# Decoder layer on one core: three of the six cross-attention units of a batch take their exponentials head by head on ScalarE, under a new written order of the work

## The reference, cut to what matters

```
q = (queries @ Wq + bq).reshape(N, L, H, D)      # L = 112 queries
k = (keys @ Wk + bk).reshape(N, S, H, D)         # S = 375 context rows
v = (values @ Wv + bv).reshape(N, S, H, D)
sm = jnp.einsum('nlhd,nshd->nlhs', q, k) / math.sqrt(D)
sm = jax.nn.softmax(sm, axis=1)                  # over l: one maximum and one sum per (h, s)
attn = jnp.einsum('nlhs,nshd->nlhd', sm, v).reshape(N, L, H * D)
```

## Time and profile before

| | |
|---|---|
| median of 3 runs (lowest, highest) | 1372.14 us (1371.88, 1373.69) |
| the profiled execution, its own time | 1372.99 us |
| its span, first to last instruction | 1371.2 us |
| PE busy | 1220.7 us (89%) |
| DVE busy | 1140.3 us (83%) |
| ACT busy | 876.9 us (64%) |
| POOL busy | 343.0 us (25%) |

### The profile page before, as it was taken

How to read it: one execution, slowest core, us unless ns; L and a number is a source line. 1 busy time by engine, 2 the same in 40 slices (tenths; PEclk the granted TensorE clock), 3 DMA queues, 4 the chain that set the end, 5 groups by cost and what they waited for, 6 DMA issues and landing times. The chain is left out here.

```text
span 1371.2 us, 28241 instructions
## 1 busy us (share of the span) xinstructions
PE 1220.7 (89%) x8850; PEld 892.6 (65%) x8850; DVE 1140.3 (83%) x2358; ACT 876.9 (64%) x2290; POOL 343.0 (25%) x431
## 2 busy tenths in 40 slices
PE   1789999999999999999999999999976868759598
PEld 1466666666666666666666666666645757659598
DVE  6369999999999999999999999999973447868698
ACT  1366666666666666666666667666532449959695
POOL 0233432233343223333222334322210000000043
PEclk9899999999999999999999999999986989979799
DMA  5100001000000100000000000000000000000033
GB/s 161 38 20 19 19 19 31 21 18 21 18 18 18 32 18 18 21 18 18 22 29 18 18 21 18 19 26 13 4 8 4 0 0 1 0 0 1 17 101 97
DMA packets 35042, 33.07 MB, mean 24 GB/s; under 512 B 4148, under 2 KB 34604, under 8 KB 34988
## 3 DMA queue, kind: packets, MB, share of 16 engines
q1 hardware_dynamic: 32704, 31.50, 7.6%
q10 hardware_dynamic: 2284, 0.89, 0.3%
HBM read 25.04 MB, written 7.34 MB: 24 GB/s over the span
## 5 line engine op out<-in xcount | busy, mean ns | idle before, releaser
L561 ACT ACTIVATE Px<-score 125x896 f32<-125x896 f32 x192 | 176.2, 918 | 127.4 <-PE score L1080 66.1
L747 DVE TENSOR_REDUCE nmax_c<-score 125x8 f32<-125x896 f32 x192 | 208.4, 1086 | 6.0 <-PE score L1002 5.6
L729 DVE TENSOR_REDUCE Zc<-Px 125x8 f32<-125x896 f32 x192 | 206.8, 1077 | 7.9 <-ACT Px L561 4.4
L554 ACT ACTIVATE Ps<-score,nmax_s 112x112 f32<-112x112 f32 x512 | 173.6, 378 | 3.6 <-DVE nmax_s L754 3.6
L506 POOL TENSOR_TENSOR rstd<-vare,half 112x1 f32<-112x1 f32 x64 | 35.0, 548 | 474.5 <-DVE vare L839 474.5
L1080 PE MATMUL score<-sel,nmaxT 128*125 128x448 f32 x384 | 125.3, 407 | 1.8 <-ACT nmaxT L567 1.8
L554 ACT ACTIVATION_READ_ACCUMULATOR Ps<-score,nmax_s 112x1 f32 x512 | 118.8, 232 | 0.0
L1091 PE MATMUL outX<-Px,Vn 125*32 125x224 f32 x1536 | 113.4, 369 | 2.1 <-DVE Vn L740 2.1
L740 DVE TENSOR_TENSOR Vn<-Vx,rZc 125x128 f32<-125x128 f32 x192 | 112.8, 587 | 1.2
L567 ACT ACTIVATE nmaxT<-maxT 128x125 fp32r<-128x125 f32 x192 | 53.6, 279 | 89.6 <-PE maxT L1074 89.4
L1002 PE MATMUL score<-Qbd_hi,KxT_hi 64*125 64x448 f32 x384 | 90.4, 467 | 1.2 <-ACT Px L561 1.2
(11 more groups left out here) (245 smaller groups left out, 3482.3 us busy)
## 6 DMA issues: line engine op xcount, KB each, us to landing
ctx_in<-in_ctx SPq DMA_DIRECT2D x32, 375.0 KB
x_in<-in_x SPq DMA_DIRECT2D x32, 112.0 KB, 2.0
x_scratch<-x SPq DMA_DIRECT2D x32, 112.0 KB, 5.6
x2T_all<-x_scratch SPq DMA_DIRECT2D x32, 112.0 KB, 2.1
out<-x2T_all SPq DMA_DIRECT2D x32, 112.0 KB, 1.9
raw_w_up<-in_w_up SPq DMA_DIRECT2D x1, 768.0 KB, 5.6
raw_w_down<-in_w_down SPq DMA_DIRECT2D x1, 768.0 KB, 7.5
raw_w_gate<-in_w_gate SPq DMA_DIRECT2D x1, 768.0 KB, 9.6
```

Of the source, the lines that this page charges most:

```text
L554: ins = act.activation(Ps[:, g, :], score[slot][0:L, h // QUAD, (h % QUAD) * L:(h % QUAD + 1) * L], ACT.Exp, bias=nmax_s[:, g:g + 1], accu ...
L561: act.activation(Px[u % 2][:].rearrange("s (q h) l -> s q (h l)", q=2), score[SLOT_OF[f"C{u}"]][0:C, :, 0:QW], ACT.Exp).then_inc(exp_c, 1)
L729: dve.tensor_reduce(Zc[p][:], Px[p][:], AX.X, ALU.add).then_inc(z_c, 1)
L747: dve.tensor_reduce(nmax_c[u % 2][:, 0:OCT].rearrange("s (q h) -> s q h", q=2), score[SLOT_OF[f"C{u}"]][0:C, :, 0:QW].rearrange("s q (h l) ...
```

## The change

Units C1, C3 and C5 (`BY_HEAD`) take the way of the self units; C0, C2 and C4 (`SHIFTED`) keep the old one. For a unit by head, DVE writes the maxima to a tile of their own (`nmax_h`), ACT runs eight exponentials of 112 columns with a bias and an accumulator output straight into `Zc`, and DVE takes the reciprocal as soon as they are done. Its transpose, copy, shift and sum are gone. The double buffers nmax_c and nmaxT now alternate over the shifted units alone.

```
+BY_HEAD = (1, 3, 5)
 SLOT_USES = (
-    (("C4", 1), ("C5", 1), ("C1", 2), ("C2", 2)),
-    (("S1", 3), ("C0", 2), ("S0", 4), ("C3", 2)),
+    (("C3", 1), ("C5", 1), ("C1", 2), ("C2", 2)),
+    (("C4", 1), ("C0", 2), ("S0", 4), ("S1", 4)),
...
+            def exp_by_head(n, u):
+                i = BY_HEAD.index(u)
+                act.wait_ge(nmax_h_done, n.times(NBH, i + 1))
+                wait(act, av_done, n.times(NU, u - 1))
+                maxima, sums = nmax_h[(n.par * NBH + i) % 2], Zc[u % 2]
+                for h in range(OCT):
+                    ins = act.activation(Px[u % 2][:, h, :],
+                                         score[SLOT_OF[f"C{u}"]][0:C, h // QUAD, (h % QUAD) * L:(h % QUAD + 1) * L],
+                                         ACT.Exp, bias=maxima[:, h:h + 1], accum_out=sums[:, h:h + 1])
+                ins.then_inc(exp_c, 1)
...
             def reciprocal_cross(n, u):
-                dve.wait_ge(z_c, n.times(NU, u + 1))
+                if u in BY_HEAD:
+                    dve.wait_ge(exp_c, n.times(NU, u + 1))
+                else:
+                    dve.wait_ge(z_c, n.shifts(SHIFTED.index(u) + 1))
...
             def max_cross(n, u):
+                if u in BY_HEAD:
+                    i = BY_HEAD.index(u)
+                    wait(dve, exp_c, n.exps(i - 2))
+                    dst, done = nmax_h[(n.par * NBH + i) % 2][:], nmax_h_done
```

More of the change, by code:

```diff
@@ L35 @@
 NU = KT * NC
+BY_HEAD = (1, 3, 5)
+SHIFTED = tuple(u for u in range(NU) if u not in BY_HEAD)
+NSH = len(SHIFTED)
+NBH = len(BY_HEAD)
 QW = QUAD * L
@@ L115, in loads, with shifts, exps @@
         return self.pair * 16 + fixed if self.looped else fixed
+    def shifts(self, i):
+        return self.times(NSH, i)
+    def exps(self, place):
+        ahead, i = divmod(place, NBH)
+        return self.times(NU, NU * ahead + BY_HEAD[i] + 1)
     def first_fills(self, use):
@@ L366, in attention @@
         nmax_c = [sb(f"nmax_c{p}", [C, P]) for p in range(2)]
+        nmax_h = [sb(f"nmax_h{p}", [C, OCT]) for p in range(2)]
         nmaxT = [sb(f"nmaxT{p}", [P, SP // NC + 1], F32R) for p in range(2)]
@@ L466, in step @@
                     save_x2(n0)
+                if n6:
+                    load_x(n6)
             iterations(sp, step)
@@ L556, in exp_self, with exp_shifted @@
                 ins.then_inc(exp_s, 1)
-            def exp_cross(n, u):
-                act.wait_ge(shifted, n.times(NU, u + 1))
+            def exp_by_head(n, u):
[8 more added lines that the diff above has]
+                ins.then_inc(exp_c, 1)
+            def exp_shifted(n, u):
+                act.wait_ge(shifted, n.shifts(SHIFTED.index(u) + 1))
                 wait(act, av_done, n.times(NU, u - 1))
@@ L564, in copy_max @@
             def copy_max(n, u):
-                act.wait_ge(nmaxT_done, n.times(NU, u + 1))
-                wait(act, shifted, n.times(NU, u - 1))
-                act.activation(nmaxT[u % 2][:, 0:C], maxT[:, 0:C], ACT.Copy).then_inc(nmaxT_copied, 1)
+                i = SHIFTED.index(u)
+                act.wait_ge(nmaxT_done, n.shifts(i + 1))
+                wait(act, shifted, n.shifts(i - 1))
+                act.activation(nmaxT[(n.par * NSH + i) % 2][:, 0:C], maxT[:, 0:C], ACT.Copy).then_inc(nmaxT_copied, 1)
             def hi_with_bias(n, use, dst, bias, done):
@@ new lines, in step @@
+                if n1:
+                    reciprocal_cross(n1, 0)
+                    normalise_values(n1, 0)
+                if n0:
+                    residual(n0, 1)
+                    moments(n0, 1)
+                if n1:
+                    reciprocal_cross(n1, 1)
+                if n2:
+                    add_eps(n2, 0)
+                if n1:
+                    max_cross(n1, 2)
+                if n2:
+                    norm_self(n2)
+                if n4:
+                    lo_with_bias(n4, "Ks", Ks[1], Ks[0], bcol["abk"], ks_hi)
@@ L916, in step @@
+                if n2:
+                    max_cross(n2, 1)
+                    sum_cross(n2, 0)
                 if n3:
[L917 to L929, removed]
@@ L930, in step @@
-                if n3:
[L931 to L945, removed]
```

395 lines of the change are left out of this document (194 added, 201 removed).

## The result

The changed kernel takes 1339.56 us (median of 4 runs, 1338.40 to 1341.01) against 1372.16 for the kernel before: ratio 0.9761, 95% interval 0.9744 to 0.9778. The forecast was 1300, a gain of 72 us; 32.6 came. The profiled execution takes 1339.93 us, its span is 1337.8, at a mean granted clock of 0.957 (before 0.964).

The account below looks back on a forecast made before the run. PE (97% busy) and VectorE (93%) were taken to bound the kernel; 29.87 us a batch falls to 27.5, and 30 batches x 2.4 = 72 us off 1372 gives 1300 us, range 1282 to 1322 (1258 to 1342 with most rivals).

Parts of the forecast that it names:

- the load of VectorE and ScalarE: Busy time per batch after the change: VectorE from 27.86 to 24.89 us, ScalarE from 19.96 to 24.64.
- the block of 125 partitions: ScalarE's eight-head block of a cross unit: 2.65 us, the self units' price, with 0 to 0.1 us more as bound.
- slots don't bind: Score slots, held from scores to exponentials: 18.0 and 17.9 us used of 27.5, so only the order could make them bind.
- the price of the meetings with POOL: VectorE's scaling of the values slowed beside GpSimd: 2.0 us a batch lost, unchanged by the new order.
- first term: PE loses three transposes and three shift pairs, 2.28 us by pitch: busy time 28.98 to 26.70 us a batch.
- leftover waits: PE's idle time remaining beside its 26.70 us of work, 0.80 us a batch, making 27.5.
- ramp and drain together as five more: Filling and emptying of the pipeline, counted as five batches that each also gain 2.4 us.
- B: Rival: VectorE was the pacer and PE's busy time padded; 26.9 us a batch, 1283 us, down to 1256; chance 0.24.
- A: The forecast itself: PE's load and leftover waits set the pace, 27.5 us a batch, 1300 us; chance 0.46.
- C: Rival: ScalarE's long blocks and more GpSimd meetings eat half the gain; 28.8 us a batch, 1340 us; chance 0.16.

Follow-up runs that it names:

- e4: Kernel before the change with GpSimd's block-diagonal products cut from 448 to 16 columns (computation left out): 1346.7 us, 28.91 us a batch.
- e3: Changed kernel with GpSimd's block-diagonal products cut from 448 to 16 columns (computation left out): 1328.2 us, 28.10 us a batch.
- e10: e4 with the pair of shifts of C1, C3 and C5 also cut to one matmul of 16 columns: 1325.3 us, 28.20 us a batch.
- e5: Changed kernel without the third product of each split score on PE (computation left out): 1336.1 us, 27.92 us a batch.
- e8: Changed kernel with VectorE's spread of the second reciprocals moved ahead of lo Qx: 1329.5 us, 28.10 us a batch.
- e11: e8 with the values product of C3 put ahead of the context's transpose on PE: 1335.0 us, 28.27 us a batch.
- e13: Changed kernel with six of eight heads in the block of C3 alone (two left out): 1333.5 us, 28.19 us a batch.
- e15: e8 with the reciprocal and scaling of C3's values also ahead of lo Qx: 1328.6 us, 28.12 us a batch.
- e1: Kernel before with C1, C3 and C5 by head but the old order, slots and work banks: 1505.8 us, 34.14 us a batch.
- e2: All six units shifted as before, in the changed kernel's order, slots and work banks: 1653.3 us, 37.73 us a batch.
- e6: Changed kernel with the three remaining sums over 56 of 112 queries (half left out): 1342.3 us, 28.42 us a batch.

## Why the prediction was wrong

**Right:** that it is faster; the load of VectorE and ScalarE to 0.1 us; the block of 125 partitions (338.27 to 340.90, 2.63 us); that slots don't bind (no wait of PE's scores for ScalarE among the changed kernel's waits in the loop). Right by luck: the price of the meetings with POOL, and VectorE's load with it. 6 x 0.11 for the scaled values, 2 x 0.37 for the spread and 0.55 for x1 are 1.9 us, where 2.0 was forecast for the scaled values alone.

**Wrong, first term:** "PE loses three transposes and three pairs of shifts ... 28.98 becomes 26.70", and from it 27.5 a batch. This is the step that failed: measured is 27.81. The pitches taken out are about right (2.06 us by the trace). But pitch is no price. From e4 to e3, between two lists that GpSimd hardly disturbs, 2.06 us went and 1.24 came back, which leaves the 0.8 above. By the distances from start to start, over ten batches, the transposes of the probabilities hold PE 2.39 us a batch instead of 1.77. Of these 0.62 us, 0.38 are idle time in e3's trace: a short piece of another chain used to stand where PE now meets a wait. e10 shows such a wait. Projections, context and x2 transposes take 0.1 to 0.2 each more, without recorded idle time, and the first product of the keys 0.3 less; why stays open.

**Wrong, second:** I treated what was left as "leftover waits" of 0.8 us on the fullest engine. Their size was not far off (0.61), but not what they are. The pace is a ring through three engines that no engine's load shows. Of the 1.45 us gained, 0.8 are PE's shorter list (28.91 to 28.10), the rest is less waiting over it (0.96 to 0.32).

**Wrong, third:** the meetings. I looked at the scaled values alone and left the sum as it was. 1.3 of the 1.9 us moved to the spread and x1, and of all these meetings the spread and one scaling stand on the ring (0.95 and 0.85 us above). The Trainium skill, "GPSIMD Engine Reference", Key points, names VectorE instructions with two SBUF inputs and those in a 2-port mode. The scaling is of the first kind, and the trace agrees (0.85 against 0.28 us). The spread is a copy (0.95 against 0.23 us) and x1's normalisation has one tensor input (0.96 against 0.41), and both are held; whether they run in that mode no row shows.

**Wrong, fourth:** "I count ramp and drain together as five more". The first maximum comes 2.9 us earlier (145.0 instead of 147.9), no more than runs of the changed lists differ among themselves (143.9 to 148.1 in e3, e5 to e8, e11 and e13 to e15); the emptying lost 11.5. Where it lost them shows when C0's exponential of the last batch is taken as a mark in between. Before, then changed:

```profile
1005.46 0.92 ACT L561 ACTIVATE Px<-score 125x896 f32<-125x896 f32 x1 [0.84 <-PE score L1080]
```

```profile
975.90 0.92 ACT L588 ACTIVATE Px<-score 125x896 f32<-125x896 f32 x1 [2.17 <-PE score L1111]
```

From the last entry to this mark 70.7 us became 84.7, 14.0 more; from there to the last exit 31.8 became 29.3, 2.5 less. So the last batch's own cross units, long blocks included, run through faster than before. What got longer is the way to them. In the new ScalarE list the copy of x stands right ahead of the exponential of C0, which the same batch reaches three steps later; in the old one it stands more than half a step behind that place. That is 84.7 / 28.42 = 3.0 batch times against 70.7 / 29.87 = 2.4. e1 and e2 tell the two halves apart: with the blocks but the old lists it is 2.3, without a block but with the new lists 3.0. I never counted how many batch times of pipeline the new order keeps behind the last entry.

**The rivals.** The rule that B takes from the Trainium skill, "Trainium Kernel Development and Optimization", Best Practices, not to judge by matmul busy time, is borne out in part: PE is 98% busy after the change, and 1.5 us less work on it gives 0.5. But B's pacer, VectorE, is not it (e6), and its time, 1283, is further off than A's. (Its lower end, 26.0 a batch, is not what 28.98 - 3.34 gives, 25.6.) C gave 1340 and 28.8 a batch. It met the total, by luck, as its loop is 0.4 us a batch too slow and it has no longer emptying; its mechanism (a block on the path of small copies, meetings at dear places) is half of what the ring is. I had it at 0.16 because I priced it by load.

## What to carry to other kernels

When several engines are nearly full (here 98, 88 and 86% in the loop), work out the ring: follow one batch's releases, each without slack, until they come back to the same instruction. The sum will always be the time of a batch, so shorten one piece on the ring and one off it to see whether it holds. Price an edit by what of it lies there, up to the next limit: 1.3 us off the ring gave nothing, 0.66 on it 0.23 a batch, 0.2 us moved off it 0.32. A removed instruction gives back its pitch only if what follows it is ready. A software pipeline's emptying is its own term: count how many batch times lie between the last entry and the last batch's own chain.

## What was not expected of the hardware

A one-input copy or normalisation on VectorE is held by GpSimd as long as a two-input one: 0.95 us for 0.23, 0.96 for 0.41. In e3, with GpSimd's products cut, both are back near their durations before the change (0.23 and 0.43 us).
